# Last attention of a four-layer kernel: split per four tiles on POOL, stacked by DMA, tiles unrolled, ones matmuls ahead of each score chunk

## What is computed

```python
h = layernorm(x)
q, k, v = split(h @ Wqkv + bqkv)              # 16 heads of 8
ka, va = split(ctx @ Wqkv_aux + bqkv_aux)[1:] # 77 context tokens
main = softmax(q @ k.T / sqrt(8)) @ v
aux  = softmax(q @ ka.T / sqrt(8)) @ va
o = (1 - sigmoid(g)) * main + sigmoid(g) * aux
x = x + tanh(gate) * (o @ Wo + bo)
```

## Time and profile before

| what | us |
|---|---|
| median of 3 runs (974.87 to 979.23) | 977.8 |
| the profiled execution | 977.78 |
| its span | 976.0 |
| busy in the span: PE, DVE, ACT, POOL | 770.9, 537.0, 340.2, 269.6 |
| experts 2 | 495.5 to 596.4 |
| attention 3 | 596.4 to 882.2 |
| experts 3 | 882.2 to 976.0 |

### The profile page before, as it was taken

One profiled execution on the slowest core, in us unless ns is written; L12 is line 12 of the kernel. 1 busy time (PEld: TensorE's weight loads), 2 busy tenths in 40 slices (PEclk: granted clock), 3 DMA queues, 4 the chain that ended last, 5 costly groups with the idle time before them and its releaser, 6 DMA issues.

```text
span 976.0 us, 15985 instructions
## 1 busy us (share of the span) xinstructions
PE 770.9 (79%) x5971; PEld 532.1 (55%) x5971; DVE 537.0 (55%) x1396; ACT 340.2 (35%) x685; POOL 269.6 (28%) x496
## 2 busy tenths in 40 slices
PE   3899999998578928545857995899988889985776
PEld 3566656665416715224553543577776667753664
DVE  2366556656530026595466463567677876636463
ACT  1444344433203300252211120345455564531244
POOL 2132333233160053001030004645445644201030
PEclk8899999999858965566558997567678986755589
DMA  8600000000112310000000002000000000000001
GB/s 256 204 1 2 1 1 1 1 1 1 41 44 69 94 43 12 0 0 1 1 0 0 1 1 86 2 1 2 1 0 0 0 0 1 2 2 1 1 1 44
DMA packets 21075, 22.37 MB, mean 23 GB/s; under 512 B 5286, under 2 KB 18075, under 8 KB 20636
## 3 DMA queue, kind: packets, MB, share of 16 engines
q1 hardware_dynamic: 18698, 19.06, 6.2%
q0 software_dynamic: 1024, 2.10, 0.7%
q10 hardware_dynamic: 1298, 0.47, 0.2%
HBM read 17.43 MB, written 4.19 MB: 22 GB/s over the span
## 4 chain that ended last, share of the span: by engine, by line
PE 41%; DVE 15%; issue 8%; ACT 6%; POOL 3%; DMA 0%; DVEq 0%; POOLq 0%
PE bank L1714 5%; PE bank L1741 4%; PE bank L1700 3%; PE bank L1813 3%; PE bank L1526 2%; PE bank L1553 2%; PE bank L1045 2%; PE bank L1726 2%; PE bank L2086 2%; PE bank L1035 2%; ACT area_b L1927 2%; DVE mx L1845 1%; PE bank L1194 1%; ACT area_b L1951 1%; PE bank L1213 1%
## 5 line engine op out<-in xcount | busy, mean ns | idle before, releaser
L1951 ACT ACTIVATE area_b<-bank 128x512 f32<-128x512 f32 (+1 forms) x128 | 72.7, 594 | 51.3 <-PE bank L1741 50.7
L1845 DVE TENSOR_REDUCE mx<-bank 128x4 f32<-128x512 f32 (+1 forms) x128 | 70.1, 579 | 27.3 <-PE bank L1726 26.7
L816 ACT ACTIVATE area_a<-area_a 128x512 f32<-128x512 f32 (+1 forms) x48 | 26.9, 562 | 121.8 <-DVE area_a L730 121.8
L1714 PE MATMUL bank<-area_b,area_a 77*32 77x128 f32 (+1 forms) x1024 | 62.4, 386 | 0.1
L608 PEld LDWEIGHTS bank<-area_a 128*128 128x128 f32 x384 | 46.7, 191 | 24.8 <-issue 24.8
L1741 PE MATMUL bank<-area_b,area_a 54*77 54x128 bf16 (+1 forms) x512 | 56.6, 251 | 4.4 <-ACT area_b L1951 4.1
L904 POOL TENSOR_TENSOR area_a<-area_a,rs 128x512 f32<-128x512 f32 (+1 forms) x48 | 40.9, 881 | 64.0 <-DVE rs L739 64.0
L608 PE MATMUL bank<-area_a 128*128 128x128 f32 x384 | 53.5, 283 | 0.0
L1741 PEld LDWEIGHTS bank<-area_b,area_a 54*77 54x77 bf16 (+1 forms) x512 | 37.0, 121 | 26.8 <-ACT area_b L1951 12.6
L1726 PE MATMUL bank<-area_a,area_b 48*128 48x77 bf16 (+1 forms) x512 | 40.8, 223 | 11.8 <-ACT area_b L1927 10.3
L2004 POOL TENSOR_TENSOR area_b<-qk,zero 128x256 bf16<-128x256 f32 (+1 forms) x32 | 23.0, 718 | 93.3 <-DVE ka L1827 93.3
(11 more groups left out here) (351 smaller groups left out, 1761.2 us busy)
## 6 DMA issues: line engine op xcount, KB each, us to landing
area_b<-in_w SPq DMA_DIRECT2D x16, 256.0 KB, 4.8
f<-in_f SPq DMA_DIRECT2D x1, 2048.0 KB
area_a<-in_f SPq DMA_DIRECT2D x1, 2048.0 KB, 8.0
x_slots<-XN SPq DMA_DIRECT2D x1, 1024.0 KB, 6.8
area_b<-x_slots SPq DMA_DIRECT2D x8, 128.0 KB, 2.4
y_slots<-area_b SPq DMA_DIRECT2D x8, 128.0 KB, 1.8
out<-X SPq DMA_DIRECT2D x1, 1024.0 KB, 4.2
X<-in_x SPq DMA_DIRECT2D x1, 896.0 KB, 12.0
```

What stands on the lines that cost most here:

```text
L1714: m = pe.matmul(SUMS3[aux][32 * j:32 * j + 32, i * 128:(i + 1) * 128], v[:, u, 4 * i + j, :], e[:, 4 * i + j, :], start=True, stop=True)
L1845: dve.tensor_reduce(mx3[:, aux, heads3(half, odd)], SCORES_RING3[j % 2][:, 0:4 * n].rearrange("p (h k) -> p h k", k=n), AX.X, ALU.max, neg ...
L1951: act.activation((ea3 if aux else em3)[:, heads3(half, odd), :], EXP_RING3[j % 2][0:n, :].rearrange("p (h q) -> p h q", q=128), ACT.Exp, s ...
```

## The change

**Layout.** Four tiles (512 tokens) are projected at once, with features in partitions: queries and keys come out of one 512-column matmul each, head pairs arranged so that a chunk's 8 features lie together (`stacked`). POOL splits 128x512 in four operations (`gpsimd_three_parts`), and SP copies parts to the stacks `qS3`, `kS3`, `kaS3` with DMAs from SBUF to SBUF, 12 a stack of 64 partitions x 1 KB each (2.4 KB for the context, all 16 tiles at once). Zero and one rows come from a new input. Scores now contract 58 rows (`SCORE_ROWS3`), shifted scores 64. Value rows are 16 floats apart, so neighbouring `sums` operands overlap.

```diff
-        bkva3 = sb("bkva3", [T, 2 * D])
+        xnT2 = carve("A", ([14920], (4, 512)), 128)
+        at3, at3b = [4096], [0]
+        qS3 = [carve("A", ([at], (8, 512)), 128, BF16) for at in (10872, 0)]
+        kS3 = [carve("A", ([at], (8, 512)), 128, BF16) for at in (17000, 2048)]
+        em3 = carve("A", (at3, (H3, 128)), 128)
+        ea3 = carve("A", (at3, (H3, 128)), T)
+        ovT3 = carve("A", (at3, (2, 4, 128)), 128)
+        v3 = [carve("A", ([at], (4 * H3 * 16 + 16,)), 128) for at in (19048, 13000)]
+        kaX3 = carve("A", ([17000], (B * T,)), 128)
+        kaS3 = carve("B", (at3b, (8, B * T)), 128, BF16)
+        va3 = carve("B", (at3b, (B * H3 * 16 + 16,)), T)
+        halves_of_xn = XN[:, :, :].rearrange("p b d -> p (b d)").bitcast(BF16)
+        kaP3 = halves_of_xn[:, 0:3 * B * T].rearrange("p (s k) -> p s k", s=3)
+        qkP3 = halves_of_xn[:, 0:6 * 512].rearrange("p (a s k) -> p a s k", a=2, s=3)
```

```diff
+        def keep_busy(pe, psum, times, n=512):
+
+            for _ in range(times):
+                pe.matmul(psum[:, 0:n], ones_b[:, :], ones_b[:, :].unsqueeze(1).to_broadcast([128, n // 128, 128]), start=True, stop=True)
+
...
+            tensor_aux3(pe)
+            pe.wait_ge(prep3_done, 7)
...
+                    if g in (1, 2) and i in (2, 3):
+                        tensor_prep3(pe, g - 1, (0, Q3)[i - 2])
+                    if g == 2 and i == 1:
+                        tensor_prep3(pe, 0, V3)
                 at_least(pe, x_updated, 5 * B + 4 * g)
...
+                    if i == 0 and g in (1, 2):
+                        vector_apply3(dve, g - 1)
...
                 act.activation(xnT2[:, g, :], GT2[:, :], ACT.Copy).then_inc(g_xnT_done, 1)
             tanh(0, 0)
             tanh(0, 1)
+            scalar_aux3(act)
             act.wait_ge(gap2_done, 1)
             act.activation(r2s["e"][:, :], r2s["d"][:, :], ACT.Exp).then_inc(gap2_done, 1)
...
+                        scalar_prep3(act, g - 2, K3)
+                    if i == 2 and g == 2:
+                        scalar_prep3(act, 0, V3)
+                    if i == 3 and g in (1, 2):
+                        scalar_prep3(act, g - 1, 0)
+                        scalar_prep3(act, g - 1, Q3)
```

In experts 0, PE gets this, and DVE the steps between:

```diff
+        def tensor_bias3(pe):
+            pe.wait_ge(ahead_step, 3)
+            pe.matmul(bank[1][0:1, 0:D], bvc3[:, :], wo3[:, :], start=True, stop=False)
+            pe.matmul(bank[1][0:1, 0:D], ones_row[:, 0:1], bo3[:, :], start=False, stop=True).then_inc(ahead_step, 1)
+            pe.wait_ge(ahead_step, 5)
+            pe.matmul(bank[1][:, D:2 * D], ones_row[:, :], bias0[:, :], start=True, stop=True).then_inc(ahead_step, 1)
+            pe.wait_ge(ahead_step, 7)
+
```

**Score chunks.** `keep_busy` puts matmuls of ones ahead of each, into the bank that the chunk then overwrites:

```diff
+            def scores(b, j):
 
                 half, aux, odd = CHUNKS3[j]
                 p, n = 64 * odd, (T if aux else 128)
-                k = (kaT3 if aux else kT3)[:, u]
                 at_least(pe, max3_done, 8 * b + j - 1)
+                if b < 2:
+                    keep_busy(pe, SCORES_RING3[j % 2], 2)
                 for i in range(4):
                     c = 4 * half + i
-                    m = pe.matmul(SCORES_RING3[j % 2][:, i * n:(i + 1) * n], qT3[p:p + PARTS3, c, :], k[p:p + PARTS3, c, 0:n],
+                    m = pe.matmul(SCORES_RING3[j % 2][:, i * n:(i + 1) * n], queries3(b, p, SCORE_ROWS3, c), keys3(b, aux, p, SCORE_ROWS3, c),
                                   start=True, stop=True)
                 m.then_inc(s3_in_psum, 1)
 
...
-                k = (kaT3 if aux else kT3)[:, u]
-                if j < 2:
-                    at_least(pe, o3_done, b)
-                else:
-                    pe.wait_ge(exp3_done, 8 * b + j - 1)
+                at_least(pe, exp3_done, 8 * b + j - 1)
+                keep_busy(pe, EXP_RING3[j % 2], 1, 256)
                 for i in range(4):
                     c = 4 * half + i
-                    m = pe.matmul(EXP_RING3[j % 2][0:n, i * 128:(i + 1) * 128], k[p:p + MAXES3, c, 0:n], qmT3[p:p + MAXES3, c, :],
+                    m = pe.matmul(EXP_RING3[j % 2][0:n, i * 128:(i + 1) * 128], keys3(b, aux, p, 64, c), queries3(b, p, 64, c),
                                   start=True, stop=True)
...
+            def turn_maxima(b):
+
+                pe.wait_ge(maxsplit3_done, b + 1)
+                at_least(pe, x_updated, 6 * B + b - 2 if b >= 2 else 0)
+                pe.transpose(MAXT3, mcol3[:, b % 2, :], ident_b[:, :]).then_inc(mT3_in_psum, 1)
+
```

**The loop of PE.** Scores run two tiles ahead; `turn_maxima` is one transpose for a tile; the sums of the context's second half run behind the next tile's first chunk:

```diff
+            for b in range(-2, B + 1):
+                work, ahead, before = 0 <= b < B, b + 2 < B, b >= 1
+                if b == -1:
+                    tensor_prep3(pe, 1, V3)
+                if b == 2:
+                    pe.wait_ge(stack3_loaded[1], STACK_LOADS + 4 * 16)
+                if ahead and b + 2 in (8, 12):
+                    pe.wait_ge(stack3_loaded[(b + 2) // 4], STACK_LOADS)
+                if work:
+                    pe.wait_ge(maxrows_loaded[b % 2], 32 * (b // 2 + 1))
+                for j in range(8):
+                    if work:
+                        scores_shifted(b, j)
+                    if ahead:
+                        scores(b + 2, j)
+                    if j == 0 and before:
+                        pe.wait_ge(exp3_done, 8 * b)
+                        for i in (2, 3):
+                            m = sums(b - 1, 1, i)
+                        m.then_inc(sums3_in_psum, 1)
+                    if j == 3 and before:
+                        turn_back(b - 1)
+                    if j == 4 and 0 <= b + 1 < B:
+                        turn_maxima(b + 1)
+                    if b in (2, 6) and j in (1, 4, 6):
+                        tensor_prep3(pe, b // 4 + 2, (0, Q3, K3)[(1, 4, 6).index(j)])
+                    if b in (4, 8) and j == 1:
+                        tensor_prep3(pe, b // 4 + 1, V3)
+                    if j == 6 and before:
+                        turn_output(b - 1)
+                    if j >= 6 and work:
+                        if j == 6:
+                            pe.wait_ge(exp3_done, 8 * b + 4)
+                            at_least(pe, o3_done, b)
+                            if b % 4 == 0:
+                                pe.wait_ge(prep3_done, block3(b // 4, V3))
+                        for i in ((0, 1), (2, 3))[j - 6]:
+                            m = sums(b, 0, i)
+                        if j == 7:
+                            m.then_inc(sums3_in_psum, 1)
+                    if j == 7 and before:
+                        output(b - 1)
+                if work:
+                    pe.wait_ge(exp3_done, 8 * b + 6)
+                    for i in (0, 1):
+                        sums(b, 1, i)
```

**ACT and POOL.** ACT also copies the sums (`turned_sums`) and evicts the projections; POOL splits the maxima in eight small operations:

```diff
+        def scalar_aux3(act):
+            for n, (psum, lo, hi) in enumerate(KA_PIECES3):
+                act.wait_ge(prep3_in_psum, n + 1)
+                act.activation(kaX3[:, lo:hi], psum[:, 0:hi - lo], ACT.Identity, bias=b3c[:, 2:3]).then_inc(prep3_done, 1)
+            act.wait_ge(pool3_done, 1)
+            for n in range(4):
+                act.wait_ge(prep3_in_psum, n + 4)
+                act.activation(va3[:, 0:B * 256].rearrange("p (j h d) -> p j h d", h=H3, d=16)[:, 4 * n:4 * n + 4, :, 0:8], VA_BANK3[n][0:T, :].rearrange("p (j h d) -> p j h d", h=H3, d=8),
+                               ACT.Copy).then_inc(prep3_done, 1)
...
+            def turned_sums(b, aux):
+                at_least(act, back3_in_psum, b)
+                act.wait_ge(sums3_in_psum, 2 * b + 1 + aux)
+                act.activation(ovT3[:, aux, :, :].rearrange("p i q -> p (i q)"), SUMS3[aux][:, :], ACT.Copy).then_inc(ovT3_done, 1)
+
...
+        def gpsimd_three_parts(pool, x, parts):
+
+            pooled(pool, pool.tensor_copy(parts[0], x))
+            pooled(pool, pool.tensor_tensor(x, x, parts[0], ALU.subtract))
+            pooled(pool, pool.tensor_copy(parts[1], x))
+            return pool.tensor_tensor(parts[2], x, parts[1], ALU.subtract)
...
+        def gpsimd_prep3(pool, g):
+            for kind in (Q3, K3):
+                pool.wait_ge(prep3_done, block3(g, kind))
+                if kind == Q3:
+                    if g == 0:
+                        pool.wait_ge(aux3_loaded, 14 * 16)
+                    else:
+                        pool.wait_ge(stack3_loaded[g - 1], STACK_LOADS + (4 * 16 if g < 3 else 0))
+                gpsimd_three_parts(pool, tmp512[:, kind - 1, :], [qkP3[:, kind - 1, i, :] for i in range(3)]).then_inc(pool3_done, 1)
+            x4 = X[:, 4 * g:4 * g + 4, :]
+            pool.wait_ge(g_xn_done, 4 * (12 + g + 1))
+            pool.tensor_tensor(x4, x4, out_bias3[:, :].unsqueeze(1).to_broadcast([128, 4, D]), ALU.add).then_inc(pool3_done, 1)
 
...
+            def split_maxima(b):
+
+                cols = mcol3[:, b % 2, :].rearrange("p (o a s c) -> p o a s c", o=2, a=2, s=3)
+                m = mx3[:, b % 2, :, :].rearrange("p a (c o) -> p o a c", o=2)
+                pool.wait_ge(max3_done, 8 * b + 8)
+                at_least(pool, mT3_in_psum, b - 1)
```

(34 more changed lines are left out.)

698 lines of the change are left out of this document (293 added, 405 removed).

## The result

The changed kernel takes 989.25 us (median of 4 runs, 986.58 to 994.15), the kernel before 976.34 on the same chip (4 runs, 971.94 to 979.23): a ratio of 1.016, 95% interval 1.0105 to 1.0214. It is slower by 1.6%. The profiled execution took 986.58 us with a span of 984.7, 8.7 us longer than the span before. The stages, cut at the last update of X in each (columns: from and to, length, then busy time of PE, PE's weight loads, DVE, ACT and POOL with counts, granted clock, DMA share, GB/s). Changed kernel: experts 0 with mixing 1, feed-forward 1, attention 2, experts 2, attention 3.

The account below looks back on a forecast made before the run. The last attention's tiles were taken as bound by PE, times 1.17 for hand-offs through two-bank rings. From 977.8 us, minus 116.0 there plus 23.7 paid elsewhere gave 886 us; own range 868 to 905, 8-in-10 range 860 to 934.

Parts of the forecast that it names:

- The new wait: Last attention: PE waits for DMAs of each tile's maxima rows; 8.3 us loop under 9.3 us tile, costed at nothing, bounds 0 to 43.
- rival (1): Last attention: the clock stays mixed, 12.2 us a tile, +46, total 932 us; chance 0.20 together with Rival (6).
- Rival (5): Last attention: PE stops at the DMA wait every tile, clock at 1.2 GHz throughout, 16.7 us a tile, 1017 us; chance 0.03.
- Rival (6): Last attention: the ones do not raise the clock at all, ending as rival (1); chance 0.20 together with it.
- PE per tile: Last attention's loop: 8.0 us of PE work a tile, times 1.17, gives 9.3 us a tile.
- The stage: Last attention: lead-in 15.5, tiles 148.8 and tail 5.5 sum to 169.8 us against 285.8, a gain of 116.0.
- Lead-in: Last attention before the first tile: 12.5 us to tile 0's transposed maxima plus 3.0 for copy and DMAs, 15.5 (12 to 25).
- The tail: End of the last attention: 5.5 us, without the bias matmul and at a better clock, against 9.4 before.
- Paid elsewhere: Stages before the last attention: costs of 23.7 us in all from work moved there.
- Keys and values of the context ahead of the router's exponential: Expert stage before the last attention: PE's sending and ACT's evictions delay the router's exponential, +6.5 us.
- DVE next to POOL's splits: Expert stage before the last attention: DVE steps slowed beside POOL's splits, 1.5 us.
- Group work: Two later groups of that expert stage: added DVE and PE work and evictions, 4.7 + 2.4 + 7.6 less 3.2 overlap, 11.5 us.

Follow-up runs that it names:

- e9: Changed kernel without the 48 DMAs loading the stacks of the third and fourth groups; tiles 8 to 15 reuse the first eight tiles' operands: 916.38 us.
- e15: e14 with a third small chained DMA, so PE's stop at tile 8 was 2.96 us: 977.66 us, stage 259.6.
- e14: e9 with one stop put back: at tile 8 PE waits for two small chained DMAs, 1.32 us: 923.74 us, stage 204.5.
- e6: Changed kernel with POOL's value-row zeroing, the router's exponential and the second group's reciprocal deviation moved, all outside the last attention: 971.68 us.
- e11: Changed kernel with the ones ahead of each shifted chunk doubled from 256 to 512 columns: 936.25 us, stage 213.9 at clock 0.91.
- e1: Changed kernel without any matmul of ones, in lead-in or loop: 946.07 us, ratio 0.971 to the kernel before.
- e10: Changed kernel with e6's moves, no ones, e4's fp32 matmuls, maxima turned earlier, later stacks in parts of 8, 12 and 4: above the expected 900 to 928 us.
- e7: Changed kernel with e6's moves, no ones, e4's fp32 matmuls and the maxima's row DMAs issued by ACT: missed its expected 905 to 920 us; total not given.
- e3: Changed kernel with the ones ahead of shifted chunks replaced by same-shape bf16 matmuls on real data: 975.14 us, stage 263.5 at clock 0.65.
- e4: Changed kernel with the loop's eight matmuls of ones a tile replaced by two fp32 ones of 384 columns: 941.63 us, stage 222.8.
- e12: Changed kernel with 256-column ones, e6's moves, maxima turned earlier, second group's and later stacks in parts: executions of 922.60 and 983.62 us, no ratio given.
- e17: e12 with the later stacks in two lots of 12 DMAs again: executions spread widely, no ratio given.
- e13: e12 with ones of 512 columns: 5 to 6% faster than the kernel before, not to be told apart from e16.
- e16: e17 with ones of 512 columns: 5 to 6% faster than the kernel before, not to be told apart from e13.

## Why the prediction was wrong

**The new wait: the step that failed.** "Costed at nothing", with 43 us as the upper bound, because the loop of 8.3 us lay 1 us under the tile. In tiles without a stack in flight that was right: none of them stopped PE for the rows. Where a stack was in flight PE stopped for 1.1 to 2.7 us (at 716 and 774 it went on 5 to 6 us behind the issue of the rows), "at worst 5 us a time" as I had it. The wait itself, 7.3 us in all, lay within my bounds. What was wrong is that I priced it in microseconds of waiting alone and left out what the clock does behind it. The stops at 716 and 774 cost 60.9 us with what followed (e9), and a stop of 2.96 us instead of 1.32 cost 55 (e15 against e14).

**The clock, rival (1), (5) and (6).** I gave 0.20 to a mixed clock, 0.03 to half clock "for the whole stage", and took the kernel to be safe since a dense PE had kept 1.00 for three tiles. It does keep it, once it has it (e9: 14 tiles). It doesn't get it back by being dense: with 256 columns of ones PE was at 1.2 GHz and 100% busy, and came back by itself only twice in all such traces (e6, e9). Rival (5) had the right mechanism, a stop and half clock behind it, but asked for a stop in every tile, where one is enough. That its tile of 16.7 us came so near the measured 16.93 is luck: it is 15.4 of work and 1.3 of waiting, and the measured tile has no waiting in it. Its turning point was 14.3 us a tile, 15.1 with the short lead-in and tail, and with 8 us more paid elsewhere the latter moves to 14.6; the measured stage stands at (263.7 − 15.8 − 8.0)/16 = 15.0, on the slower side. Rival (6) was right that 256 columns of ones do next to nothing for the clock, and wrong for 512 (e11); that it would then end as (1), at 932, was wrong too, since the ones themselves cost 33 us of the stage (e1).

**PE per tile.** 8.0 us times 1.17 was 9.3; measured 9.92 busy in 10.13 (e9) in a tile without group work, for which my terms give 7.5, so PE does more and is hindered less than I had it. Without ones it is 8.2 busy in 9.32 us (e1), where my terms give 6.6; the ones I had at 0.9, and they are 1.7 of busy time and 0.8 of the tile. At half clock 15.4 was 1.5 too low.

**The stage.** Lead-in 15.5: tile 0's first shifted chunk started at 644.94, 15.8 behind the opening. The tail, 5.5: from the last sums to the last update it took 8.0 us at half clock, 6.1 at full (e9). With the clock held from tile 2 on the stage is 202.8 (e9), 33 us above my 169.8: some 13 of it from tiles 2 to 14, and most of the rest from the stretch ahead of them, much of which ran at half clock behind the first two stops (1.12 and 2.03 us there).

**Paid elsewhere.** Predicted 23.7, measured about 32. Keys and values of the context ahead of the router's exponential: +6.5 predicted, +6.6 measured (the exponential comes 30.5 us behind the opening for 23.9). DVE next to POOL's splits: 1.5 predicted, 3.1 measured for the router. Group work: 11.5 predicted; the two groups took 21.6 and 29.8 us for 17.8 each, 15.8 more, the second through POOL's order, a wait I had not seen. Of that sum's terms, 4.7 is the DVE work of both groups and 7.6 the PE work and evictions, but 2.4 is not derived from anything; without it the prediction would have been 9.1. The bias chain: 3.2 predicted, 3.7 measured. The memset: 1.0 predicted "where POOL is idle", 4.1 measured, for four memsets; I asked whether POOL was free and not whether DVE was. The last weights at nothing: right, experts 3 are no longer than before.

## What to carry to other kernels

When work is taken off the other engines until PE is the bound, price every wait left on PE by what TensorE's clock does behind it and for how long, not by its length: here 1.6 us more of idle PE cost 55 us, and a kernel that did more useless work was the faster one because it recovered and stopped for less. Put a stop into the kernel yourself, take several executions, and look at the granted clock behind it before believing in a filler. And an instruction moved to an idle POOL is not free: look at what DVE does in those microseconds.

## What the runs showed of the hardware

- TensorE can stay at 1.2 GHz with PE busy 16.93 of 16.93 us a tile, for over 100 us. The same instructions, once at 2.4 GHz, stayed there for 14 tiles (e9).
- In the new loop every one of 22 stops of PE of over 1.75 us at full clock was followed by a fall to 1.2 GHz. Falls also came behind shorter ones, down to 0.60 us (e10), while 1.32 (e14) and 1.71 us (e7) had none.
- Ones or real data made no difference for the clock (e3), and what fp32 work did for it (e4), bf16 ones did too when they had twice the columns (e11).
- The granted clock of the same code differs between executions: attention 2 took 43.0 us at 0.78 (e9) and 51.5 at 0.57 (e7), and the full kernels with 256 columns of ones (e12, e17) spread over 50 to 61 us in all, those with 512 (e13, e16) over 12 to 19. The changed kernel's four executions lay within 8.
- Four POOL memsets in a row, the longest of 77 rows and 4112 columns, held up DVE's normalisations by 4.1 us, and beside a POOL tensor instruction of 2.64 us a DVE step of 0.28 lasted 2.60.
- Small DMAs on a second queue came later (4.2 to 5.9 us of waiting for 1.1 to 2.7) than behind the stacks on the same queue.
